# A decoder layer with routed experts on one core: routing's last row sends and its two counts are moved

## The chip, the cores and the metric

The kernel runs on one core of one Trainium2 chip. Times are device microseconds (us) of a whole execution; lower is better. Three runs of the kernel before took 683.22, 685.04 and 685.03 us, a median of 685.03. The execution that the profiler recorded took 685.55 us, of which 683.7 us lie between its first and last instruction (the span). Engines are called PE (TensorE), DVE (VectorE), ACT (ScalarE), POOL (GpSimd) and SP (SyncE, which here only issues transfers and loads registers from memory).

## The reference

Input x has 64 sequences of 64 tokens with 128 features, so 4096 rows, or 32 tiles of 128 rows. The layer does three things in a row: self-attention and a layer norm, cross-attention to a context and a layer norm, and a mixture of experts with a final layer norm. What matters here is the last part:

```python
t = (x * rsqrt(mean(x * x) + 1e-5) * norm_scale).reshape(4096, 128)
logits = t @ gate_w + gate_b                   # 8 experts
top_v, top_i = top_k(logits, 2)                # each row goes to 2 of them
probs = softmax(top_v)
h = swiglu(t @ w1[e] + b1[e])                  # 128 -> 512 -> 256
y = h @ w2[e] + b2[e]                          # 256 -> 128
x = layernorm(x + sum of probs * y over the row's two experts)
```

## The kernel before, in words

The kernel has two stages. In the first, attention and cross-attention run over the 32 tiles as a software pipeline: every engine has its own instruction list, written as one slot per step (`slot(at)`), with waits on semaphores between the engines. A cross-attention step works on several tiles at once, each at its own lag: at step s the layer norm's scale is made for tile s-10 (POOL, L1012, then the residual's bias for tile s-9, L1017), the normed row for tile s-11 (DVE, L1153), the router's logits for tile s-14. There are 60 such steps, 0 to 59; the last tile's scale is made at step 41, and steps 42 to 49 only finish the routing.

Routing collects tiles in batches of 8, 8, 4, 4, 4 and 4. For a batch, DVE chooses two experts per row in four phases (L1089 to L1174), PE sums how many rows went to each expert so far (L887 to L893), and DVE makes each row's place in a table in memory sorted by expert (`x_pos`, L1131, semaphore `placed`). POOL then sends the rows there: `send_row` issues indirect transfers of 128 rows each (L778, `disp_dram<-l_R,x_pos`), two for a tile, one for each choice. A list made when the program is built, `scatter_at`, says how many at which step; what is left (`late`, tiles 24 to 31) is sent inside the next stage.

The rows are sorted in two parts: tiles 0 to 19 are the first, 20 to 31 the second. When a part's batches are counted, PE makes the totals (`tally`, L917) and DVE a table of which block of 128 sorted rows belongs to which expert (`count`, L1197, and `table`, L1203 to L1218; SP stores it, L768). For the second part this is followed by two instructions that make `l_c`, a factor per row.

The second stage runs over 48 pairs of blocks of 128 sorted rows. For a pair, SP loads two table entries into registers (`find`, L1327) and issues two loads of 128 rows (`m_blk<-disp_dram`, L1339); for the first pair it first waits until the first part's 40 sends have landed (`scattered[0]`). PE loads the two experts' numbers (`load_experts`, L1370), turns the blocks (`turn_rows`, L1378), and multiplies (L1397, L1403, then L1412, L1422, and L1433 to turn the middle result). DVE divides a turned pair into a high and a low part (`split`, L1556 and L1561), then makes `m_lin` (L1610), `m_pr` (L1615) and the product (L1622). POOL sends the results (L1535). Before its loop PE turns pairs 0 and 1, and inside the loop pair p+2 behind the first products of pair p; DVE likewise splits pairs 0 and 1 first, and pair p+2 between `m_pr` and the product of pair p. All orders are written out by hand; each engine runs its list strictly in that order.

Of the kernel before, what the change touches and what calls it, by code (L numbers as in the profile page):

```python
# [641 lines left out]
def cross_attention(nc, ctx, ps, x1, x1_stored, ctxT, biases, disp, block_table, tiles, later):  # L642
# [7 lines left out]
    BATCHES = ((0, 8), (8, 8), (16, 4), (20, 4), (24, 4), (28, 4))  # L650
# [3 lines left out]
    part_of = lambda B: 0 if B < firsts else 1  # L654
    scatter_at, sent = {}, 0
    for step in range(tiles + LAG):
        placed_tiles = sum(n for t, n in BATCHES if step >= t + n + 18)
        some = min(placed_tiles - sent, 1 if step < tiles + 10 else 4) if step < tiles + 14 else 0
        scatter_at[step] = range(sent, sent + some)
        sent += some  # L660
    late = range(sent, tiles)
    def sb(name, shape, dt=F32):
        return ctx.enter_context(nc.sbuf_tensor("x_" + name, shape, dt))

# [92 lines left out]
    def step_of(at):  # L757

        return at[0] * U + at[1]
# [7 lines left out]
        sp.wait_ge(table_made, 2 * part + 2)  # L767
        sp.dma_start(block_table[part * P:part * P + P, :], eri[:, part, :]).then_inc(later.table_stored[part], 16)  # L768

    def send_row(pool, t):  # L770

        B = batch_of[t]
        j = t - BATCHES[B][0]
        if t == 0:
            pool.wait_ge(later.pattern_made, 3)
        pool.wait_ge(placed, B + 1)
        for k_ in range(2):
            nc.gpsimd.indirect_dma_start(  # L778
                out=disp[:, :], out_offset=bass.IndirectOffsetOnAxis(ap=pos[:, B, k_, j:j + 1], axis=0),
                in_=R[:, t, k_, :], in_offset=None).then_inc(scattered[part_of(B)], 16)  # L780

    def sync(sp):
        def slot(at):
# [16 lines left out]
    def tensor(pe):  # L800
# [7 lines left out]
        def slot(at):  # L808
# [64 lines left out]
            before = Tile(at, 8)  # L873
            if before.live:
                before.wait(pe, normed)
            if step_of(at) == tiles + 10:
                pe.wait_ge(tally_read, 1)
            if o.live:
                o.free(pe, lg_kept, 1)
# [2 lines left out]
            if z.t in last_of:  # L882
# [11 lines left out]
                                            ohs[:, B % 2, i, :].unsqueeze(1).to_broadcast([P, size - 1 - i, 8]),  # L894
                                            start=False, stop=(i == size - 2), skip_group_check=True)
                last.then_inc(ranked, 1)
            if step_of(at) == tiles + 9:
                tally(0)
            if o.live:
                if o.t == 0:  # L900
# [11 lines left out]
        def tally(part):  # L912

            B = (firsts, len(BATCHES))[part]
            pe.wait_ge(rank_read, B)
            pe.wait_ge(counted, B + 1)
            nc.tensor.matmul(ps_cnt, later.onesb[:, :], cum[:, B + part, :], start=True, stop=True).then_inc(tallied, 1)  # L917

        return slot, lambda: tally(1)

    def scalar(act):
        def slot(at):
# [68 lines left out]
    def gpsimd(pool):  # L991
        G = nc.gpsimd
        pool.wait_ge(later.filled, later.all_filled)

        def slot(at):
            c, h, k, w = (Tile(at, n) for n in (3, 9, 10, 2))
            if c.live:
                if c.t == 0:
                    pool.wait_ge(prepared, 4)
                c.wait(pool, k_ready)  # L1000
                c.free(pool, scored, 3)
                G.tensor_tensor(  # L1002
                    KB[:, c.t % 3, :, :, :],
                    kT[:, c.u4, :].rearrange("p (b k) -> p b k", b=2).unsqueeze(2).to_broadcast([P, 2, 8, T]),
                    hm[:, :].unsqueeze(1).unsqueeze(3).to_broadcast([P, 2, 8, T]),
                    ALU.mult).then_inc(k_spread, 1)
            if k.live:
                k.wait(pool, ln_var)
                if k.t == 0:
                    G.iota(R[:, :, :, P:P + 1].rearrange("p t k o -> p t (k o)").bitcast(I32), [[1, tiles], [CAP, 2]],  # L1010
                           base=0, channel_multiplier=32).then_inc(later.pattern_made, 1)
                G.tensor_tensor(later.rs[:, k.t, :], ve[:, k.u2, :], later.halfneg[:, 0:2],  # L1012
                                ALU.pow).then_inc(ln_rstd, 1)
            if h.live:
                h.wait_ring(pool, xb_in, 16)
                h.free(pool, y_added, 2)
                G.tensor_tensor(xr[:, h.u2, :], xb[:, h.u2, :], bob[:, :], ALU.add).then_inc(residual, 1)  # L1017
            if 0 <= w.t < 8:
                e = w.t
                pool.wait_ge(W1_cut, e + 1)  # L1020
                G.tensor_tensor(later.W1l[:, e, :], later.W1[:, e, :], W1c[:, e % 2, :],
                                ALU.subtract).then_inc(later.W1_low, 1)
            for t in scatter_at[step_of(at)]:
                send_row(pool, t)
        return slot, lambda: None

    def vector(dve):
# [16 lines left out]
        def slot(at):  # L1044
# [16 lines left out]
            if o.live:  # L1061
# [1 line left out]
                oB = batch_of[o.t]  # L1063
                V.tensor_tensor(lg[:, oB % 2, o.t - BATCHES[oB][0], :], ps_lg, later.gb[:, :],
                                ALU.add).then_inc(lg_kept, 1)
            if step_of(at) == tiles + 10:
                count(0)
            if rank:
                yB = last_of[y.t]
# [119 lines left out]
            if w.t == 18:  # L1189
                dve.wait_ge(B_part, 2)  # L1190
                V.tensor_tensor(Brest[:, 1, :], Brest[:, 0, :], Bpart[:, 1, :], ALU.subtract).then_inc(B_rest, 1)
            if step_of(at) == tiles + 10:
                table(0)
        def count(part):

# [30 lines left out]
            n.settle()  # L1226
            n.add(V.scalar_tensor_tensor(later.c2[:, :], later.rs[:, :, 0], 2.0, later.c2[:, :], ALU.mult, ALU.mult))

        return slot, end

    return sync, tensor, scalar, gpsimd, vector, store_table, late, send_row

# [1 line left out]
def experts(nc, ctx, ps, disp, block_table, Y, out, tiles, later, store_table, late, send_row):  # L1234
# [54 lines left out]
    def part_of(p):  # L1289

        return 0 if p < PA else 1
# [70 lines left out]
    def tensor(pe):  # L1362
# [19 lines left out]
        load_experts(1)  # L1382
        turn_rows(0)
        turn_rows(1)
        for s in range(PAIRS + 2):
            p, q, u = s, s - 2, s - 1
            if p < PAIRS:
# [123 lines left out]
    def gpsimd(pool):  # L1511
# [15 lines left out]

        for q in range(PAIRS):
            for t in late[0:3] if q == 0 else late[3 + q // 2:4 + q // 2] if q % 2 else ():
                send_row(pool, t)  # L1530
            pool.wait_ge(y_ready, q + 1)
            if q >= 4:
                pool.wait_ge(*landed(q - 4))
# [12 lines left out]
    def vector(dve):  # L1546
# [58 lines left out]

        split(0)
        split(1)
        for p in range(PAIRS):
            dve.wait_ge(up, p + 1)
            n.add(V.tensor_scalar(lin[:, :, :], ps_l[:, p % 2, :, :], -6.0, 8.0, ALU.max, ALU.min))  # L1610
# [146 lines left out]
```

## Time and profile before

| | |
|---|---|
| median of three runs | 685.03 us (683.22 to 685.04) |
| the profiled execution | 685.55 us, span 683.7 us |
| busy, share of the span | PE 78%, DVE 72%, POOL 65%, ACT 63% |
| last steps of the first stage (414 to 438 us) | DVE busy 16.57 of 24 us, POOL 19.84, PE 15.16 |
| from there to the first expert products (438 to 469 us) | PE busy 3.15 of 31 us, DVE 11.38, POOL 23.27 |
| the stretch from 482.4 to 640 us | PE busy 138.46 of 157.6 us |

Busy time is not the same as what sets the end: between 438 and 469 us no engine but POOL has much to do, and the time passes in waits. A timeline row gives the start, the duration, the engine, the line of the kernel and, in brackets, how long the engine stood idle before it and what ended that. The chain of waits follows the work that ended last back from the end, and names at each moment the engine or transfer it hung on.

### The profile page before, as it was taken

To read this page: it belongs to the slowest core of one execution; us is meant where nothing else is said; L and a number is where in the kernel's file an instruction comes from. 1 tells how busy PE (TensorE), PEld (TensorE's weight loads), DVE (VectorE), ACT (ScalarE), POOL (GpSimd) and SP (SyncE) were. 2 spreads that over 40 slices of the span, in tenths; PEclk is the share of its full clock that TensorE was granted. 3 is DMA by queue.
4 is the path that set the end of the run, shared out by engine and by line. 5 is a ranking of instruction groups with operands and counts; after the bars stand their busy time and mean duration, and the time that the engine had idled before them with its cause. 6 is when DMAs were issued, how large, how long until landed. Compare 5 with 4: busy or idle time off the path is not lost.

```text
span 683.7 us, 18235 instructions
## 1 busy us (share of the span) xinstructions
PE 535.7 (78%) x5390; PEld 415.6 (61%) x5390; DVE 489.7 (72%) x1696; ACT 430.6 (63%) x1287; POOL 445.9 (65%) x475
## 2 busy tenths in 40 slices
PE   7678779688886769999989888403887899999962
PEld 3456656566665646777756666302776788888830
DVE  3689896689998776878898987732554666678813
ACT  3799888789996759778756654101434555555633
POOL 6678796678896596566558886873265445456742
PEclk9899998899998989999999989555899999999998
DMA  2255655745222111111112111121222222252144
GB/s 58 88 196 192 231 192 160 259 122 144 51 58 63 54 47 33 37 35 49 37 34 59 36 33 45 44 61 49 55 63 65 63 63 64 55 178 62 47 117 121
DMA packets 72528, 58.48 MB, mean 86 GB/s; under 512 B 22866, under 2 KB 66012, under 8 KB 70386
## 3 DMA queue, kind: packets, MB, share of 16 engines
q1 hardware_dynamic: 67250, 47.79, 23.9%
q0 software_dynamic: 4608, 8.47, 3.8%
q10 hardware_dynamic: 576, 1.05, 0.5%
q8 instruction: 48, 0.79, 0.5%
q14 instruction: 46, 0.38, 0.2%
HBM read 26.39 MB, written 31.92 MB: 85 GB/s over the span
## 4 chain that ended last, share of the span: by engine, by line
PE 31%; issue 19%; POOL 15%; ACT 10%; DVE 9%; DMA 8%; SPq 6%; another core or an unknown queue 1%; ACTq 0%; DVEq 0%; POOLq 0%
PE ps L1397 9%; POOL l_keys L1002 6%; DMA l_shifted<-in_xT 5%; ACT l_weights L359 5%; PE ps L1422 4%; POOL disp_dram L778 4%; PE ps L1403 2%; PE ps L320 2%; POOL l_rs L1012 2%; PE ps L1433 2%; SPq L242 2%; POOL x_xr L1017 2%; PE ps L290 1%; PE ps L313 1%
## 5 line engine op out<-in xcount | busy, mean ns | idle before, releaser
L1535 POOL DMA_INDIRECT y_dram<-l_keys,m_blk x80 | 79.4, 992 | 89.3 <-ACT l_keys L1485 71.1
L359 ACT ACTIVATE l_weights<-ps,a_nb,a_rinv 128x64 f32<-128x64 f32 x256 | 99.5, 414 | 4.5 <-DVE a_nb L480 3.7
L778 POOL DMA_INDIRECT disp_dram<-l_R,x_pos x64 | 63.1, 987 | 17.5 <-issue 17.0
L446 POOL TENSOR_TENSOR a_rinv<-a_ms,a_halfneg 128x10 f32<-128x10 f32 (+1 forms) x32 | 62.5, 1953 | 11.0 <-DVE a_ms L512 8.9
L1610 DVE TENSOR_SCALAR m_lin<-ps 128x512 f32<-128x512 f32 x40 | 27.7, 692 | 50.7 <-PE ps L1403 48.0
L320 PE MATMUL ps<-l_R,l_shifted 128*128 128x512 f32 x64 | 40.5, 717 | 28.2 <-DMA l_shifted<-in_xT 19.7
L1002 POOL TENSOR_TENSOR l_keys<-x_kT,l_table 128x1024 f32<-128x1024 f32 x32 | 61.1, 1908 | 0.2
L1485 ACT ACTIVATE l_keys<-ps,m_blk 128x128 f32<-128x128 f32 x80 | 25.0, 363 | 49.6 <-PE ps L1422 33.3
L359 ACT ACTIVATION_READ_ACCUMULATOR l_weights<-ps,a_nb,a_rinv 128x1 f32 x256 | 55.2, 216 | 0.0
L1012 POOL TENSOR_TENSOR l_rs<-x_ve,l_halfneg 128x2 f32<-128x2 f32 x32 | 25.6, 799 | 39.9 <-DVE x_ve L1149 39.3
L412 POOL TENSOR_TENSOR l_R<-l_weights,a_pa 128x512 f32<-128x512 f32 x32 | 33.5, 1046 | 26.3 <-DVE a_pc L574 24.4
L1397 PE MATMUL ps<-l_W1h,m_th 128*128 x160 | 37.8, 318 | 15.1 <-issue 9.2
L1422 PE MATMUL ps<-l_table,l_keys 128*128 x320 | 43.1, 277 | 4.9 <-ACT l_keys L1498 3.3
L1477 ACT ACTIVATE l_weights<-ps 128x512 f32<-128x512 f32 x40 | 23.9, 598 | 35.9 <-PE ps L1403 32.7
L1105 DVE TENSOR_REDUCE x_mx<-ps 128x16 f32<-128x1024 f32 x32 | 39.0, 1219 | 7.8 <-PE ps L832 7.8
L1422 PEld LDWEIGHTS ps<-l_table,l_keys 128*128 128x128 f32 x320 | 38.8, 191 | 6.4 <-issue 6.4
L1397 PEld LDWEIGHTS ps<-l_W1h,m_th 128*128 128x128 f32 x160 | 26.2, 196 | 23.9 <-issue 23.8
L832 PE MATMUL ps<-l_keys,x_qT 64*64 64x512 f32 x256 | 36.4, 640 | 5.2 <-DVE l_shifted L1127 4.8
L932 ACT ACTIVATE l_weights<-l_shifted 128x1024 f32<-128x1024 f32 x32 | 33.6, 1050 | 10.0 <-DVE l_shifted L1127 9.9
L1127 DVE TENSOR_TENSOR l_shifted<-ps,x_mx 128x1024 f32<-128x1024 f32 x32 | 38.7, 1208 | 0.2
L909 PE MATMUL ps<-l_VB,x_PT 128*64 128x32 f32 x1024 | 36.8, 226 | 0.6 <-ACT x_PT L937 0.6
L332 PE MATMUL ps<-l_R,l_W1h 128*128 128x256 f32 x128 | 36.0, 405 | 1.3 <-ACT l_R L347 1.3
(229 smaller groups left out, 1728.6 us busy)
## 6 DMA issues: line engine op xcount, KB each, us to landing
disp_dram<-l_R SPq DMA_DIRECT2D x16, 1040.0 KB, 4.4
m_blk<-disp_dram SPq DMA_DIRECT2D x80, 65.0 KB
l_shifted<-in_xT SPq DMA_DIRECT2D x32, 64.0 KB, 3.9
l_W1h<-v_dram SPq DMA_DIRECT2D x128, 16.0 KB, 2.3
l_R<-in_x SPq DMA_DIRECT2D x32, 64.0 KB, 2.1
x_dram<-a_xo SPq DMA_DIRECT2D x32, 64.0 KB, 1.7
l_W1l<-in_w SPq DMA_DIRECT2D x4, 512.0 KB
x_xa<-x_dram SPq DMA_DIRECT2D x32, 64.0 KB, 1.8
```

The costliest lines, as they stand in the source:

```text
L320: nc.tensor.matmul(flat[:, 0:512], xTt[:, a.u2, :], wqkv[:, 0:512], start=True, stop=True)
L359: last = nc.scalar.activation(E[:, e.u4, g, :], ps_Sh[:, g % 2, g // 2, 0:D], ACT.Exp, bias=nb[:, e.u2, g:g + 1], scale=rinv[:, e.u4, g:g ...
L446: G.tensor_tensor(rinv[:, b.u4, 0:w], ms[:, b.u2, 0:w], halfneg[:, 0:w], ALU.pow).then_inc(inv_rms, 1)
L778: nc.gpsimd.indirect_dma_start(out=disp[:, :], out_offset=bass.IndirectOffsetOnAxis(ap=pos[:, B, k_, j:j + 1], axis=0), in_=R[:, t, k_, :] ...
L909: last = nc.tensor.matmul(ps_O[T * q:T * q + T, c, :], PT[:, c, T * q:T * q + T], VB[:, f.u4, q, c, :], start=True, stop=True)
L1002: G.tensor_tensor(KB[:, c.t % 3, :, :, :], kT[:, c.u4, :].rearrange("p (b k) -> p b k", b=2).unsqueeze(2).to_broadcast([P, 2, 8, T]), hm[: ...
L1012: G.tensor_tensor(later.rs[:, k.t, :], ve[:, k.u2, :], later.halfneg[:, 0:2], ALU.pow).then_inc(ln_rstd, 1)
L1105: n_mx = n.add(V.tensor_reduce(mx[:, :], ps_S, AX.X, ALU.max))
L1127: V.tensor_tensor(sh[:, d.u2, :, :], ps_S, mx[:, :].unsqueeze(2).to_broadcast([P, H, T]), ALU.subtract).then_inc(shifted, 1)
L1397: nc.tensor.matmul(dst[:, p % 2, j, :], left, right[:, bass.ds(e, 1), half * I:(half + 1) * I].rearrange("p a n -> p (a n)"), start=(i == ...
L1422: last = nc.tensor.matmul(ps_y[:, j, :], hT[:, q % 2, 2 * j + c, :], W2[:, bass.ds(expert[2 * q + j], 1), c, :].rearrange("p a n -> p (a n)"),
L1535: G_.indirect_dma_start(out=Y[:, :], out_offset=bass.IndirectOffsetOnAxis(ap=blk[:, (2 * q + j) % NB, P:P + 1].bitcast(I32), axis=0), in_= ...
```

## The change

Three edits, with no instruction added or removed.

1. Sends are now counted in single transfers and not in tiles. Up to step 34 there are two a step as before; from step 35 to 41 three a step; from step 42 up to eight. Transfers 0 to 38 are then sent by step 41 (before: 0 to 31), 39 to 46 at step 42 (before: 32 to 39), 47 at step 43 (before: 40 to 47). The late ones stay.
2. The first part's total (PE), its `count` and its `table` (DVE) stand three steps sooner: PE at step 38, DVE at step 39.
3. The second part's total stands on PE behind the turn of pairs 0 and 1, and its count, table and `l_c` on DVE behind the split of pairs 0 and 1, ahead of the first `m_lin`.

```diff
-        placed_tiles = sum(n for t, n in BATCHES if step >= t + n + 18)
-        some = min(placed_tiles - sent, 1 if step < tiles + 10 else 4) if step < tiles + 14 else 0
+        placed_rows = 2 * sum(n for t, n in BATCHES if step >= t + n + 18)
+        most = 2 if step < tiles + 3 else 3 if step < tiles + 10 else 8 if step < tiles + 14 else 0
+        some = min(placed_rows - sent, most)
         scatter_at[step] = range(sent, sent + some)
         sent += some
-    late = range(sent, tiles)
+    late = range(sent // 2, tiles)
...
-    def send_row(pool, t):
+    def send_row(pool, row):
+        t, k_ = row // 2, row % 2
...
-        for k_ in range(2):
-            nc.gpsimd.indirect_dma_start(
+        nc.gpsimd.indirect_dma_start(
...
     def tensor(pe):
-            if step_of(at) == tiles + 10:
+            if step_of(at) == tiles + 7:
                 pe.wait_ge(tally_read, 1)
-            if step_of(at) == tiles + 9:
+            if step_of(at) == tiles + 6:
                 tally(0)
-        return slot, lambda: tally(1)
+        later.last_tally = lambda: tally(1)
+        return slot, lambda: None
...
     def vector(dve):
-            if step_of(at) == tiles + 10:
+            if step_of(at) == tiles + 7:
                 count(0)
-            if step_of(at) == tiles + 10:
+            if step_of(at) == tiles + 7:
                 table(0)
-        return slot, end
+        later.last_table = end
+        return slot, lambda: None
...
         turn_rows(0)
         turn_rows(1)
+        later.last_tally()
...
         split(0)
         split(1)
+        later.last_table()
```

The program's order on POOL, at the last steps of the first stage: `l_rs` and `x_xr` open a step's work, the sends close it. Before:

```order
L1012 TENSOR_TENSOR l_rs<-x_ve,l_halfneg 128x2
L1017 TENSOR_TENSOR x_xr<-x_xb,x_bob 128x128
L778 DMA disp_dram<-l_R,x_pos 33024x130 x2
L1012 TENSOR_TENSOR l_rs<-x_ve,l_halfneg 128x2
L778 DMA disp_dram<-l_R,x_pos 33024x130 x24
L1535 DMA y_dram<-l_keys,m_blk 8192x128 x2
```

And in the changed kernel:

```order
L1014 TENSOR_TENSOR l_rs<-x_ve,l_halfneg 128x2
L1019 TENSOR_TENSOR x_xr<-x_xb,x_bob 128x128
L779 DMA disp_dram<-l_R,x_pos 33024x130 x3
L1014 TENSOR_TENSOR l_rs<-x_ve,l_halfneg 128x2
L779 DMA disp_dram<-l_R,x_pos 33024x130 x18
L1540 DMA y_dram<-l_keys,m_blk 8192x128 x2
```

Each of steps 35 to 40 has a third send, and the run that closes step 41 (3, 8, 1 and the first 6 late ones) has 18 and not 24.

On DVE, between the last place of routing (`x_pos`) and the first `m_lin` of the experts, before:

```order
L1131 CAST x_pos<-x_posf 128x2x4
L1197 TENSOR_SCALAR x_ni<-ps 128x8
L1203 TENSOR_SCALAR x_nbi<-x_ni 128x8
...
L1218 TENSOR_SCALAR x_eri<-x_er,l_table 128x1
L1225 RECIPROCAL l_c<-l_rs 128x32
L1227 SCALAR_TENSOR_TENSOR l_c<-l_rs,l_c 128x32
L1556 TENSOR_SCALAR m_tTc<-ps 128x256
L1561 TENSOR_TENSOR m_tl<-ps,m_tTc 128x256
L1556 TENSOR_SCALAR m_tTc<-ps 128x256
L1561 TENSOR_TENSOR m_tl<-ps,m_tTc 128x256
```

And in the changed kernel:

```order
L1133 CAST x_pos<-x_posf 128x2x4
L1561 TENSOR_SCALAR m_tTc<-ps 128x256
L1566 TENSOR_TENSOR m_tl<-ps,m_tTc 128x256
L1561 TENSOR_SCALAR m_tTc<-ps 128x256
L1566 TENSOR_TENSOR m_tl<-ps,m_tTc 128x256
L1199 TENSOR_SCALAR x_ni<-ps 128x8
L1205 TENSOR_SCALAR x_nbi<-x_ni 128x8
...
L1220 TENSOR_SCALAR x_eri<-x_er,l_table 128x1
L1227 RECIPROCAL l_c<-l_rs 128x32
L1229 SCALAR_TENSOR_TENSOR l_c<-l_rs,l_c 128x32
L1616 TENSOR_SCALAR m_lin<-ps 128x512
```

The thirteen instructions of the second count now stand between the split of pair 1 and the first `m_lin`.

On PE the total `ps<-x_cum,l_onesb 128x8` of the second part stood ahead of the expert numbers' loads:

```order
L893 MATMUL ps<-x_ohs,l_onesb 128x8
L917 MATMUL ps<-x_cum,l_onesb 128x8
L1370 TENSOR_LOAD block_table
...
L1378 MATMUL ps<-l_table,m_blk 128x128 x4
L1397 ISA
```

and now stands behind both turns (the x4 are pairs 0 and 1):

```order
L894 MATMUL ps<-x_ohs,l_onesb 128x8
L1373 TENSOR_LOAD block_table
...
L1381 MATMUL ps<-l_table,m_blk 128x128 x4
L918 MATMUL ps<-x_cum,l_onesb 128x8
L1401 ISA
```

It can run only once pair 1's rows are there, since PE takes its list in order.

## Rows read from the trace of the kernel before

**Rows 1.** The page: shares of the chain that ended last, by engine.

```profile
PE 31%; issue 19%; POOL 15%; ACT 10%; DVE 9%; DMA 8%; SPq 6%; another core or an unknown queue 1%; ACTq 0%; DVEq 0%; POOLq 0%
```

**Rows 2.** Chain of waits, 444 to 476 us: start us, us, what.

```profile
440.49 3.58 DMA block_table<-x_eri
...
447.30 4.83 issue
...
452.29 0.36 SPq L1339
...
453.14 0.70 SPq L1339
...
471.38 0.69 SPq L1327
...
472.60 0.15 SPq L1327
...
473.54 1.87 DMA m_blk<-disp_dram
```

**Rows 3.** Timeline of PE, 441 to 479 us: start us, us, instruction, [idle before].

```profile
445.57 0.22 PE L893 MATMUL ps<-x_ohs,l_onesb 128*128 128x24 bf16 x3
446.79 0.17 PE L917 MATMUL ps<-x_cum,l_onesb 128*128 128x8 bf16 x1 [1.00 <-issue]
455.14 0.69 PE L1378 MATMUL ps<-l_table,m_blk 128*128 128x128 f32 x2 [8.18 <-DMA m_blk<-disp_dram]
468.77 0.69 PE L1378 MATMUL ps<-l_table,m_blk 128*128 128x128 f32 x2 [12.95 <-DMA m_blk<-disp_dram]
```

**Rows 4.** Timeline of POOL, 412 to 490 us.

```profile
417.00 0.96 POOL L778 DMA_INDIRECT disp_dram<-l_R,x_pos  x1 [0.30 <-issue]
418.88 0.82 POOL L1012 TENSOR_TENSOR l_rs<-x_ve,l_halfneg 128x2 f32<-128x2 f32 x1 [0.92 <-DVE x_ve L1149]
...
422.64 0.73 POOL L1012 TENSOR_TENSOR l_rs<-x_ve,l_halfneg 128x2 f32<-128x2 f32 x1
...
437.36 0.73 POOL L1012 TENSOR_TENSOR l_rs<-x_ve,l_halfneg 128x2 f32<-128x2 f32 x1
...
449.84 0.95 POOL L778 DMA_INDIRECT disp_dram<-l_R,x_pos  x1 [0.30 <-issue]
...
467.52 0.96 POOL L778 DMA_INDIRECT disp_dram<-l_R,x_pos  x1 [0.30 <-issue]
```

**Rows 5.** Timeline of DVE, 412 to 490 us.

```profile
431.31 0.29 DVE L1086 TENSOR_TENSOR x_r<-ps,x_xr 128x128 f32<-128x128 f32 x1 [1.93 <-POOL x_xr L1017]
...
438.63 0.17 DVE L1203 TENSOR_SCALAR x_nbi<-x_ni 128x8 int32<-128x8 int32 x1
...
447.32 0.16 DVE L1197 TENSOR_SCALAR x_ni<-ps 128x8 int32<-128x8 f32 x1
...
451.10 0.22 DVE L1227 SCALAR_TENSOR_TENSOR l_c<-l_rs,l_c 128x32 f32<-128x32 f32 x1 [0.95 <-DVE l_c L1225]
...
469.96 0.42 DVE L1561 TENSOR_TENSOR m_tl<-ps,m_tTc 128x256 fp32r<-128x256 f32 x1
472.64 0.69 DVE L1610 TENSOR_SCALAR m_lin<-ps 128x512 f32<-128x512 f32 x1 [2.25 <-PE ps L1403]
...
476.10 0.42 DVE L1556 TENSOR_SCALAR m_tTc<-ps 128x256 uint32<-128x256 uint32 x1 [2.04 <-PE ps L1378]
```

**Rows 6.** Busy time of each engine, granted clock and DMA share by stretch.

```profile
core 0: us, PE busy (x) PEld busy (x) DVE busy (x) ACT busy (x) POOL busy (x), PEclk, DMA share, GB/s
451.00:469.00 18.00, 0.91 (x3) 0.52 (x4) 1.07 (x3) 0.42 (x1) 13.41 (x14) 0.50 0.24 67
...
475.60:482.40 6.80, 5.53 (x25) 4.86 (x25) 2.64 (x5) 1.31 (x3) 0.00 (x0) 0.50 0.27 45
```

**Rows 7.** Chain of waits, 476 to 500 us.

```profile
477.33 2.93 PE ps L1397 x12
...
486.91 1.75 PE ps L1397 x12
```

More of the change, by code:

```diff
@@ L768, in store_table @@
         sp.dma_start(block_table[part * P:part * P + P, :], eri[:, part, :]).then_inc(later.table_stored[part], 16)
-    def send_row(pool, t):
+    def send_row(pool, row):
+        t, k_ = row // 2, row % 2
         B = batch_of[t]
         j = t - BATCHES[B][0]
-        if t == 0:
+        if row == 0:
             pool.wait_ge(later.pattern_made, 3)
         pool.wait_ge(placed, B + 1)
-        for k_ in range(2):
-            nc.gpsimd.indirect_dma_start(
-                out=disp[:, :], out_offset=bass.IndirectOffsetOnAxis(ap=pos[:, B, k_, j:j + 1], axis=0),
-                in_=R[:, t, k_, :], in_offset=None).then_inc(scattered[part_of(B)], 16)
+        nc.gpsimd.indirect_dma_start(
+            out=disp[:, :], out_offset=bass.IndirectOffsetOnAxis(ap=pos[:, B, k_, j:j + 1], axis=0),
+            in_=R[:, t, k_, :], in_offset=None).then_inc(scattered[part_of(B)], 16)
     def sync(sp):
@@ L1022, in slot @@
                                 ALU.subtract).then_inc(later.W1_low, 1)
-            for t in scatter_at[step_of(at)]:
-                send_row(pool, t)
+            for row in scatter_at[step_of(at)]:
+                send_row(pool, row)
         return slot, lambda: None
@@ L1529, in gpsimd @@
             for t in late[0:3] if q == 0 else late[3 + q // 2:4 + q // 2] if q % 2 else ():
-                send_row(pool, t)
+                send_row(pool, 2 * t)
+                send_row(pool, 2 * t + 1)
             pool.wait_ge(y_ready, q + 1)
```

## The prediction

> **What bounds the kernel now.** I read four views, in this order. The page's chain of waits comes first: it hangs on PE for 31% and on POOL for 15%, and 19% of it is "issue", time in which the engine at its head waited for nothing that the profile shows [rows 1]. So there is no single bound; the end is the sum of stages, and a change in one stage is worth what that stage gets shorter. Second, the chain in order of time between 444 and 476 us, where the change acts. There it runs through SP and not through a computing engine: SP has its table entries, stands for 4.83 us, issues pair 0's first load at 452.29 us, and then each instruction of its list shows about 0.70 us, from 453.14 to 471.38 us; right after that the same register operation takes 0.15 us [rows 2]. I call this stretch the slow spell. Third, PE's timeline: it is through with routing at 446.79 us, stands 8.18 us for pair 0's rows and 12.95 us more for pair 1's, which it turns at 468.77 us [rows 3]. No product can start before, since PE turns both pairs first. Fourth, POOL's timeline in the same time: it sends without a break up to 467.52 + 0.96 us [rows 4]. From 451 to 469 us PE, DVE and ACT are each busy for about 1 us or less of 18, POOL for 13.41, the rest of POOL's time being the gap that each send has before it [rows 6].
>
> So what bounds this stretch is the first part's 40th send. It is the one at 449.84 us, the last of step 42; SP's first load follows at 452.29, 2.45 us later [rows 2, 4]. Behind it, SP's slow spell sets when pair 1's rows come.
>
> **Edit 1, three sends a step.** What one send costs: the sends at 449.84 and 467.52 us are 14 apart, (467.52 - 449.84) / 14 = 1.263 us from start to start [rows 4]. Seven of them move from steps 42 and 43 to steps 35 to 41. If the steps had room for them, the 40th send would go out 7 x 1.263 = 8.8 us sooner; if they had none, not at all. These are the two ends. The rows tell which is near. POOL had 0.92 us idle ahead of step 36's scale (418.88 us) and none ahead of the one of step 37 (422.64 us) [rows 4]; and at 431.31 us it is DVE that stood 1.93 us for POOL's `x_xr` [rows 5]. From step 36 on POOL is the engine the others wait for, so a third send there only makes the step longer. Idle time that a third send can fill: the 0.92 us behind step 35's sends. The longer idle time ahead of step 35's scale lies before the first added send and stays. The gain is 0.92 us: the 40th send goes at 449.84 - 0.92 = 448.9 us, SP's first load at 451.4.
>
> What is late in exchange: step 41's scale stands behind six added sends now, 6 x 1.263 - 0.92 = 6.7 us later, at 437.36 + 6.7 = 444.0 us [rows 4]. DVE's steps 42 to 49 follow it, and with them PE's last sums, 445.57 + 6.7 = 452.2, less 1.9 us for the table that no longer stands among those steps (438.63 to its store at 440.49 [rows 2, 5]): 450.4 us. Then PE loads four experts' numbers; before, this ended well inside the 8.18 us that it stood [rows 3]. Even if it took 4 us it would be over at 454.4, against 455.14 - 0.92 = 454.2 for pair 0's turn: a tie, and harmless, because the products wait for pair 1's turn 13 us later. I take 0 for it. Every batch's places are made before POOL comes to the sends that need them.
>
> At this place the Trainium skill has a rule on how POOL is to be read. Its page "Perfetto Trace Analysis", section "GPSIMD Instruction", says that a GpSimd instruction's span in a profile is unreliable and is better timed by the spacing of starts. The rows bear it out: 0.95 to 0.96 us of span against 1.263 us of spacing. By spans the ends would be 6.7 us and 0, and the value taken would be the same 0.92.
>
> **The slow spell.** After step 42's first send there are 7 + 1 + 6 = 14 more, and behind step 42's last there were 8 + 6 = 14 before. So between SP's first load and the end of POOL's sends the program has the same list on both engines as before, all 0.92 us sooner. Pair 1's turn moves with it, to 467.9 us, and so does pair 2's load, whether the spell ends with the sends or lasts for a number of SP's instructions. This edit is worth -0.9 us to the end.
>
> **Edit 2, the first count three steps sooner.** The table's store goes from 440.49 to about 434 us. SP then stands longer for the 40 sends; the 4.83 us before [rows 2] become some 10. Worth 0. Its cost, 1.9 us of DVE at step 39, lies ahead of DVE's next wait for POOL, which was 1.93 us there [rows 5] and grows by 1.26 with the third send. Queued behind PE's wait for the reading of the total are the logits and the last products of step 39; they wait for one DVE instruction that stands early in the step. 0.
>
> **Edit 3, the second count behind pair 1.** Thirteen DVE instructions. They took from 447.32 to 451.10 + 0.22 us = 4.0 us before, with two unusual pauses; the same table for the first part took 1.9 us, with the count and the factor some 2.4 [rows 2, 5]. So between 2.4 and 4.0 us, and I take the dearer. Before, they stood in DVE's idle time ahead of pair 0, so taking them away gives nothing. At the new place: DVE ends pair 1's split at 469.96 + 0.42 - 0.92 = 469.5 us, the count ends at 473.5 at the latest, and the first `m_lin` starts there and not at 472.64 - 0.92 = 471.7. It is up to 1.8 us late. Behind it stand `m_lin` and `m_pr`, 2 x 0.7 = 1.4 us, and then pair 2's split, which waited 2.04 us for PE's turn and started at 476.10, now 475.2 [rows 5]. 473.5 + 1.4 = 474.9: through with 0.3 us to spare, 1.9 us with the cheaper value. ACT uses `l_c` only behind pair 2's split. The cover is that wait for pair 2's rows, and if it were gone, up to 4.0 us would stand open. On PE the total is one short product, 0.17 us [rows 3], ahead of pair 0's products: 0.2 us at most, within the rounding. Worth 0.
>
> **Sum.** -0.9 + 0 + 0 = -0.9 us. Against the profiled execution: 685.55 - 0.9 = 684.6, span 682.8. That execution is 0.5 us above the median, so for the median 685.03 - 0.9 = 684.1 us. From 482.4 us on nothing is changed, and the stretch moves as a whole.
>
> **The rivals.**
> *The slow spell gets shorter.* Before, SP's first load came some 11 sends into an unbroken run of 24; now it comes 5 sends into one of 18. If the spell needs a long run behind it, SP's loads for pair 1 are issued fast. For it: SP's steps were not slow in the steps with two sends. Against it: it began right behind SP's own first load, not at a number of sends. Without any spell, pair 1's rows come 2.5 us behind pair 0's and not 468.77 - 455.14 = 13.6; PE would turn them at about 457 us, 12 us sooner, and the second count's open time would be made up by pair 2's rows coming sooner too: 673 us. With half of it: 679. The Trainium skill speaks for a spell that has another cause: "DMA: Bandwidth & Descriptors", section "Issuing engines are not separate DMA queues", says that all transfers interleave on the same 16 engines whoever issues them. By it the sends could delay SP's data, hardly its register operations, and with a DMA share of 0.24 in the stretch [rows 6] not by much. The spell would then stay or go for reasons outside the sends; the time would be one of the two, 684.1 or 673.
>
> *The half clock lasts longer, and the kernel is slower.* The granted clock is at 0.50 (1.2 GHz) from 451 to 469 us, after little PE work, and still from 475.6 to 482.4 us [rows 6]. Twelve products take 2.93 us there and 1.75 us at full clock [rows 7]. Steps 36 to 41 now leave PE idler, and the level may return later. A pair costs 1.2 us more in these products and as much again, at most, in its turns and the rest: two more pairs at half clock are +3.8 us, so 685.03 - 0.9 + 3.8 = 687.9. It decides from the second such pair on; one alone gives +1.0, within 0.3%. Against it: the idle stretch ahead of pair 1 has the same length as before, and the steps that get idler end long before it.
>
> *It does what it says and POOL had room after all.* If a send costs less than 1.26 us of a step because DVE's chain is the longer one in steps 36 to 40, up to 8.8 us would be gained: 676 us. The rows at 422.64 and 431.31 us speak against it.
>
> **How the numbers follow.** About what this kernel's measurement can tell from no change is 0.3%, 2.1 us. Chances: my forecast 0.62, with an own range of 682.5 to 686; the shorter spell 0.20, a third of it as its full form; the longer half clock 0.14; room on POOL 0.04. Faster by over 0.3%: 0.20 + 0.04 and 0.06 of my forecast's spread, 0.30. Slower by over 0.3%: 0.14 and 0.02 of that spread, 0.16. Within: 0.54. The range leaves out the full form of the shorter spell and the far end of the half clock: 678 to 687.5.
>
> **What would show it.** Right: in the changed kernel the run behind step 41's scale has 18 sends; the scales of steps 36 to 41 stand about 5 us apart (before 3.7); SP's first `m_blk` load comes near 451.4 us; SP shows 0.70 us again; PE turns pair 1 near 467.9; DVE's second count ends about a microsecond or two behind PE's first products, and pair 2's split still waits for PE. Wrong: pair 1's turn before 465 us; SP's register operations at 0.15 us while POOL sends; DVE reaching pair 2's split later than its turn; a granted clock of 0.50 past 485 us.

## The result and the profile after

Both kernels were run 20 times in turn on one chip. The kernel before took 682.77 us (median, 678.88 to 685.67), the changed one 679.76 us (673.67 to 684.45): a ratio of 0.9954 with a 95% interval of 0.9932 to 0.9976. It is faster by 3.1 us, give or take 1.5. I had forecast 0.9 us. Repeated later on chip 2, 12 runs of the changed kernel had a median of 677.63 us against 683.44 for the one before, a ratio of 0.9921 (0.9887 to 0.9955). Both gains have the forecast's sign and are larger than forecast. The chip matters, as the experiments show, so each run below is named with its chip; the number of the first comparison's chip is not on record, and I call it the first chip. Ratios are of fast executions alone and are estimated together with their interval, so they can be up to 0.2% off the quotient of the medians.

The profiled execution of the changed kernel took 677.33 us, with a span of 675.5. Single executions of one kernel differ by 4 us before the change even begins to act: step 35's scale on POOL stands at 414.23 us in the first trace of before and at 410.05 in a second one; in this trace of the changed kernel it stands at 410.13. So all comparisons below count from step 35's scale. The second stage has 40 pairs, 0 to 39 (the traces have 40 `m_lin`), and not 48 as I wrote ahead of the prediction.

The chain's shares (the page, as [rows 1]). POOL's share fell from 15% to 12%, DMA's from 8% to 5%:

```profile
PE 33%; issue 20%; POOL 12%; ACT 11%; DVE 9%; SPq 6%; DMA 5%; another core or an unknown queue 2%; DVEq 0%; ACTq 0%; POOLq 0%
```

The timeline of POOL, which answers to [rows 4]:

```profile
415.16 0.73 POOL L1014 TENSOR_TENSOR l_rs<-x_ve,l_halfneg 128x2 f32<-128x2 f32 x1
...
420.06 0.74 POOL L1014 TENSOR_TENSOR l_rs<-x_ve,l_halfneg 128x2 f32<-128x2 f32 x1
...
439.84 0.73 POOL L1014 TENSOR_TENSOR l_rs<-x_ve,l_halfneg 128x2 f32<-128x2 f32 x1
...
444.76 0.96 POOL L779 DMA_INDIRECT disp_dram<-l_R,x_pos  x1 [0.30 <-issue]
...
462.43 0.96 POOL L779 DMA_INDIRECT disp_dram<-l_R,x_pos  x1 [0.30 <-issue]
```

The scales stand 4.9 us apart with no idle time ahead of them; before, it was mostly 3.7. The 40th send comes 444.76 - 410.13 = 34.63 us behind step 35's scale; before, 449.84 - 414.23 = 35.61. That is 0.98 us sooner.

The chain of waits in order of time, which answers to [rows 2, 7]:

```profile
429.77 0.32 SPq L769
...
435.81 11.30 issue
...
447.27 0.36 SPq L1342
...
448.52 0.70 SPq L1342
...
461.19 0.69 SPq L1342
...
462.58 2.95 DMA m_blk<-disp_dram
...
467.78 2.92 PE ps L1401 x12
```

The first table is stored at 429.77 us and SP stands 11.30 us for the sends, not 4.83. Its first load then goes out 2.51 us behind the 40th send (2.45 before). From 448.52 us on SP shows the 0.70 us again.

The timeline of PE, as [rows 3]:

```profile
446.40 0.22 PE L894 MATMUL ps<-x_ohs,l_onesb 128*128 128x24 bf16 x3
451.06 0.69 PE L1381 MATMUL ps<-l_table,m_blk 128*128 128x128 f32 x2 [4.44 <-issue]
457.31 0.69 PE L1381 MATMUL ps<-l_table,m_blk 128*128 128x128 f32 x2 [5.56 <-DMA m_blk<-disp_dram]
457.79 0.21 PE L918 MATMUL ps<-x_cum,l_onesb 128*128 128x8 bf16 x1
...
465.90 0.69 PE L1381 MATMUL ps<-l_table,m_blk 128*128 128x128 f32 x2 [4.38 <-DMA m_blk<-disp_dram]
```

Here is what I had not forecast. Pair 0's turn stands where it was (40.93 us behind step 35's scale, 40.91 before), but pair 1's follows 6.25 us later and not 13.63.

The timeline of DVE, as [rows 5]:

```profile
458.49 0.42 DVE L1566 TENSOR_TENSOR m_tl<-ps,m_tTc 128x256 fp32r<-128x256 f32 x1
458.83 0.15 DVE L1199 TENSOR_SCALAR x_ni<-ps 128x8 int32<-128x8 f32 x1
...
461.13 0.26 DVE L1229 SCALAR_TENSOR_TENSOR l_c<-l_rs,l_c 128x32 f32<-128x32 f32 x1
466.27 0.69 DVE L1616 TENSOR_SCALAR m_lin<-ps 128x512 f32<-128x512 f32 x1 [4.88 <-remote]
```

The second count takes 461.39 - 458.83 = 2.56 us and is through while PE makes pair 0's products, whose last group begins at 460.57 and runs 0.95 us. But `m_lin` starts only at 466.27. "remote" means that the wait ended with nothing that the profile can name. The trace's semaphore events can: PE's increment of `up` is recorded at 466.25 us, 4.73 us behind the end of the matmul that carries it, and the slow spell on SP is over at 466.1. Part of the time won is lost again there. `m_lin` of pair 0 starts 56.14 us behind step 35's scale (58.41 before), pair 1's 61.49 (66.95), and the end comes at 265.40 (269.52).

The busy time by stretch, as [rows 6]:

```profile
core 0: us, PE busy (x) PEld busy (x) DVE busy (x) ACT busy (x) POOL busy (x), PEclk, DMA share, GB/s
447.00:457.30 10.30, 0.69 (x2) 0.29 (x2) 1.96 (x9) 0.42 (x1) 7.65 (x8) 0.50 0.32 78
457.30:461.20 3.90, 3.89 (x18) 3.58 (x19) 2.89 (x15) 1.70 (x2) 2.91 (x4) 0.50 0.15 51
461.30:464.60 3.30, 0.22 (x2) 0.00 (x0) 0.09 (x1) 0.00 (x0) 1.78 (x2) 1.00 0.27 81
464.70:471.40 6.70, 4.31 (x19) 3.64 (x20) 2.73 (x5) 1.31 (x3) 0.00 (x0) 0.50 0.18 40
```

Two sets of twelve products run at a granted clock of 0.50 (1.2 GHz), one before and one after a short full stretch, as in the kernel before. The half clock doesn't last longer.

### The profile page after: what moved, and what is told of

Same layout as the page of the kernel before. It is cut to its first block, busy times and chain, and to the rows that moved or that the text cites. A ratio compares the mean times of both kernels' runs of the same rounds, so it can differ in the third digit from the quotient of the medians.

```text
span 675.5 us, 18237 instructions
## 1 busy us (share of the span) xinstructions
PE 536.7 (79%) x5390; PEld 417.1 (62%) x5390; DVE 489.1 (72%) x1696; ACT 430.4 (64%) x1287; POOL 445.9 (66%) x475
## 4 chain that ended last, share of the span: by engine, by line
PE 33%; issue 20%; POOL 12%; ACT 11%; DVE 9%; SPq 6%; DMA 5%; another core or an unknown queue 2%; DVEq 0%; ACTq 0%; POOLq 0%
PE ps L1401 8%; POOL l_keys L1004 6%; ACT l_weights L359 6%; PE ps L1426 4%; DMA l_shifted<-in_xT 4%; PE ps L1407 3%; POOL disp_dram L779 2%; PE ps L320 2%; PE ps L1437 2%; SPq L242 2%; PE ps L313 2%; PE ps L290 2%; PE ps L302 2%; POOL x_xr L1019 1%
## 5 line engine op out<-in xcount | busy, mean ns | idle before, releaser
L910 PE MATMUL ps<-l_VB,x_PT 128*64 128x32 f32 x1024 | 38.4, 231 | 0.8 <-ACT x_PT L939 0.6
L939 ACT ACTIVATE x_PT<-ps 128x1024 f32<-128x1024 f32 x32 | 32.6, 1017 | 8.7 <-PE ps L822 8.2
```

Of the source, the lines that this page charges most:

```text
L910: last = nc.tensor.matmul(ps_O[T * q:T * q + T, c, :], PT[:, c, T * q:T * q + T], VB[:, f.u4, q, c, :], start=True, stop=True)
```

## The experiments

Twelve runs on three chips. The table has medians; "end" is the end of the profiled execution, counted from step 35's scale. In the first chip's traces it is 269.52 us for before and 265.40 for after.

| run | chip | us | before, same chip | ratio (95%) | end |
|---|---|---|---|---|---|
| edit 1 alone | 3 | 682.93 | 683.07 | 1.0007 (0.9974-1.0040) | 272.42 |
| edits 2 and 3 alone | 3 | 682.26 | 683.07 | 0.9987 (0.9952-1.0021) | 277.34 |
| changed, late rows one a pair | 3 | 683.71 | 683.07 | 1.0016 (0.9988-1.0043) | 271.79 |
| changed, with pauses | 3 | 670.65 | 683.07 | 0.9823 (0.9783-0.9863) | 258.65 |
| before, with pauses | 7 | 649.60 | 650.91 | 0.9996 (0.9959-1.0033) | 238.97 |
| changed, pauses, second count early | 7 | 649.96 | 650.91 | 0.9976 (0.9936-1.0017) | 237.31 |
| changed, every second pause | 7 | 649.53 | 650.91 | 0.9971 (0.9933-1.0010) | 238.19 |
| changed, late sends paused too | 7 | 651.33 | 650.91 | 1.0004 (0.9967-1.0040) | 239.94 |
| changed, again | 2 | 677.63 | 683.44 | 0.9921 (0.9887-0.9955) | 267.55 |
| before, with pauses, again | 2 | 677.08 | 683.44 | 0.9894 (0.9844-0.9945) | 262.50 |
| before against itself | 3 | 681.73 | 682.73 | 1.0006 (0.9973-1.0039) | 274.84 |
| changed, with pauses, again | 3 | 668.17 | 682.73 | 0.9797 (0.9754-0.9840) | 258.96 |

**Edit 1 alone.** The counts stay where they were.

```diff
-            if step_of(at) == tiles + 7:
+            if step_of(at) == tiles + 10:
                 count(0)
```

> The changed kernel with its first edit alone: three sends a step, both counts where they were before. Theory 1 (the gain comes from POOL's sends: the 40th one is 0.9 us sooner and the unbroken run behind it is 18 long and not 24, which makes SP's slow spell shorter) expects the whole gain here: about 3 us under the kernel before, SP's first row load 0.9 us sooner counted from step 35's scale, and pair 1 turned at least 3 us sooner counted the same way. Theory 2 (the gain comes from taking the second count out of DVE's and PE's lists ahead of pair 0) expects the kernel before's time, within 1 us.

Measured: no gain, 1.0007. The trace shows where it goes. Its 40th send comes as early as in the changed kernel (34.65 us behind step 35's scale), but the longer steps delay the first table. The chain of waits:

```profile
441.60 0.32 SPq L769
...
448.73 0.69 SPq L1340
...
449.45 0.70 SPq L1340
```

The table's store goes out 441.60 - 408.74 = 32.9 us behind step 35's scale (26.3 before, 19.6 in the changed kernel). SP has then to read it, and its first load comes at 40.71, 6.06 us behind the 40th send and not 2.5. So in this trace edit 1 needs edit 2. The medians alone do not settle it, as the changed kernel without pauses was never timed on chip 3. And SP shows 0.69 us here at 448.73 us already, before its first load is out: the spell does not begin with that load.

**Edits 2 and 3 alone.**

```diff
-        most = 2 if step < tiles + 3 else 3 if step < tiles + 10 else 8 if step < tiles + 14 else 0
+        most = 2 if step < tiles + 10 else 8 if step < tiles + 14 else 0
```

> The changed kernel with both moved counts, but two sends a step up to step 41 as before. Theory 1 expects no gain: within 1 us of the kernel before, SP's slow spell as long as before, the second count hidden by DVE's wait. Theory 2 expects 3 us less than before.

Measured: 0.9987, no gain that can be told from none. Its 40th send is late, 39.02 us behind step 35's scale where the first trace of before had 35.61. Two steps are longer than in that trace; the same is seen below in two traces of kernels without edit 1.

**Late rows one a pair.** In five of the loop's pairs POOL has four sends in a row, and ACT waits up to 3.1 us for "remote" there. Here each pair gets one late row at most.

```diff
+            first = 2 * late[0]
+            for row in range(first, first + 6) if q == 0 else range(first + 5 + q, first + 6 + q) if q < 11 else ():
+                send_row(pool, row)
```

> The changed kernel, but the ten late row sends that went out two at a time behind the results of pairs 0, 2, 4, 6 and 8 go out one at a time, behind the results of pairs 0 to 9. In both traces PE's semaphore increments come about 2 to 2.5 us late in each of the five pairs with two row sends, which follow two result sends: four sends in a row. Theory A (it takes four sends at 1.26 us from start to start to build this up) expects that no increment is late with three in a row: up to 5 x 2 = 10 us less than the changed kernel. Theory B (what counts is how many row sends there are, wherever they stand) expects the same time within 1 us, with ten smaller delays.

Measured: 1.0016, 4 us slower by the ratio than the changed kernel was on the first chip; part of that may be the chip. Up to `m_lin` of pair 0 it is like the changed kernel (56.28 us), and from pair 1's to pair 39's it takes 169.6 us where the two traces of the changed kernel have 166.9 and 166.6. Increments still come 1 to 3.7 us late, most of them in every second pair. Four sends in a row are not the condition.

**The changed kernel with pauses.** An addition that nobody reads (0.41 us) stands behind the sends of rows 39 to 53.

```diff
+        if 39 <= row < 54:
+            nc.gpsimd.tensor_tensor(pause[:, row - 39, :], bob[:, :], bob[:, :], ALU.add)
```

> The changed kernel with a small POOL addition (128x128 into a buffer that nobody reads) behind each of rows 39 to 53's sends, so that these sends stand about 1.7 us apart and not 1.26, while SP loads pairs 0 and 1. Number of sends and of SP's instructions unchanged. Theory A (the sends' pace at 1.26 us makes SP slow) expects SP's register operations at their 0.15 us, pair 1 turned 3 to 6 us sooner than in the changed kernel counted from step 35's scale, and 2 to 5 us less in total. Theory C (SP is slow in this stretch whenever any sends are under way, or for its own loads' sake) expects pair 1's turn where it was or later, and the time within 1 us or longer.

Measured: 0.9823, 12.4 us faster than before. The timeline of POOL:

```profile
444.18 0.41 POOL L785 TENSOR_TENSOR x_pause<-x_bob 128x128 f32<-128x128 f32 x1
444.76 0.98 POOL L781 DMA_INDIRECT disp_dram<-l_R,x_pos  x1 [0.17 <-issue]
445.77 0.41 POOL L785 TENSOR_TENSOR x_pause<-x_bob 128x128 f32<-128x128 f32 x1
446.35 0.98 POOL L781 DMA_INDIRECT disp_dram<-l_R,x_pos  x1 [0.17 <-issue]
```

and of PE:

```profile
450.06 0.69 PE L1385 MATMUL ps<-l_table,m_blk 128*128 128x128 f32 x2 [4.71 <-issue]
451.57 0.69 PE L1385 MATMUL ps<-l_table,m_blk 128*128 128x128 f32 x2 [0.82 <-DMA m_blk<-disp_dram]
```

The sends start 1.585 us apart and not 1.263; POOL is through 4.4 us later, and pair 1's turn follows pair 0's after 1.5 us. The spell on SP is gone but for a few instructions. PE's late increments are not: four of them, of matmuls that end between 470.8 and 472.5 us, are recorded 3.8 to 5.3 us late, and `m_lin` of pair 4 waits 6.34 us for "remote".

**The kernel before with pauses, and three variants of the paced kernel.** These four ran on chip 7.

> The kernel before with the same pause (a 128x128 addition on GpSimd) behind the sends of rows 39 to 53, so that they stand 1.585 us apart there too. If the slow spell comes from the sends' pace, it goes here as well, and what is left between this kernel and the paced changed one is the worth of the three edits without the spell. Theory P (the edits are worth what the blind sum said, 0.92 us of sends, less the second count, which now stands open for some 2 us): this kernel at 683 - 12 = 671, within 1.5 us of the paced changed kernel's 670.65. Theory Q (the three edits themselves are worth the measured 3 us): 674. Theory R (the shorter run of sends is what made the changed kernel quicker, and the pause does the same for both): 671, and pair 1's turn 1.5 to 2.5 us behind pair 0's.

```diff
+            if 39 <= 2 * t + k_ < 54:
+                nc.gpsimd.tensor_tensor(pause[:, 2 * t + k_ - 39, :], bob[:, :], bob[:, :], ALU.add)
```

> The paced changed kernel with the second part's count back at the end of routing (edit 3 undone). There PE and DVE turn and split pair 0 and 1 at once and the count's 2.6 us are no longer hidden behind a wait for rows. If it was open in the paced kernel, moving it back ahead of pair 0's rows, into idle time, makes m_lin of pair 0 start 2 to 2.6 us sooner and the kernel 2 us faster, about 668.5. If the first m_lin's start is set by PE's products (11 us behind the turn) or by pair 2's rows, nothing is gained: 670.6.

```diff
-        later.last_table = end
-        return slot, lambda: None
+        return slot, end
```

> The paced changed kernel with the pause behind every second send only (rows 39, 41, ... 53): pairs of sends 1.26 us apart, 1.42 us on the mean. If the spell depends on the mean pace with a limit between 1.26 and 1.42, it is gone and the time is 670 or a little less, since POOL is through 2.2 us sooner. If only the full 1.585 us lets the queue drain, SP shows 0.70 us again for a part of the stretch and the time lies between 672 and 679.

```diff
-        if 39 <= row < 54:
+        if 39 <= row < 54 and row % 2:
```

> The paced changed kernel with the pause behind the late sends too (rows 39 to 63, the ten in the loop included). In the five pairs of the loop with two row sends, four sends follow each other at 1.27 us and two pairs took 10.2 us where others took 8.2. If pace is the cause there as well, this costs nothing on POOL, which waits 3 us for ACT once every two pairs, and gains up to 5 x 2 = 10 us: 661. If those 2 us have another cause (ACT's or PE's own work), 670 to 671; if POOL becomes late by its pauses, 1 to 2 us slower.

```diff
-        if 39 <= row < 54:
+        if 39 <= row < 64:
```

Measured: the kernel before, without any pause, takes 650.91 us on this chip, 32 us less than on the others, and none of the four differs from it by more than its interval. Most of my expectations miss, as they took the spell for a property of the program. Up to step 35's scale all is as long as elsewhere (407.45 to 411.48 us here, 408.51 to 414.23 on the others). What is missing is the lateness. I matched each of PE's 684 semaphore increments with its own record in the trace. In the first trace of before 28 are recorded over 0.7 us behind their matmul and 35 have no record of their own, in the one of the changed kernel 38 and 34, and over all ten traces of the other chips 28 to 50 and 28 to 55. In the four traces of chip 7 none is late, and 0, 2, 0 and 0 have no record. In each of the ten, PE's first missing record stands 1.5 to 1.7 us behind POOL's first send of rows, at 358.3 to 363.2 us, and none is late or missing before it.

The pauses do not change this on a chip that has it: the two traces of the changed kernel with pauses on chip 3 have 38 and 40 late increments and 55 and 43 without a record. So the late increments and SP's slow list are two things, and only the second went with the pauses. All four kernels profiled on chip 7 have pauses; the kernel before without any was timed there and not profiled, but it is as quick as they are. And all runs on chip 7 were made in one session, so what is said of the chip could be of the occasion. From `m_lin` of pair 1 to that of pair 39 it is 150.4 us in the paced kernel before, against 166.4 in the first trace. The page shows it in how long POOL stood idle ahead of its sends of results (behind the second bar: in all, and what of it ended with ACT's results), for the kernel before on the first chip (first fence) and with pauses on chip 7 (second):

```profile
L1535 POOL DMA_INDIRECT y_dram<-l_keys,m_blk x80 | 79.4, 992 | 89.3 <-ACT l_keys L1485 71.1
```

```profile
L1540 POOL DMA_INDIRECT y_dram<-l_keys,m_blk x80 | 80.0, 1000 | 50.7 <-ACT l_keys L1490 31.2
```

The same on SP's timeline. Its first ten loads of rows take 26.64 us on the first chip in the kernel before, and 11.63 us on chip 7 in the kernel with every second pause, though sends 1.26 us apart are among them:

```profile
452.29 26.64 SPq L1339 DMA_DIRECT2D m_blk<-disp_dram  x10
```

```profile
448.57 11.63 SPq L1346 DMA_DIRECT2D m_blk<-disp_dram  x10
```

Is it the rows' data? The trace's packets of the software queue speak against it: on the first chip and on chip 7 the first packet of a send leaves mostly 1.53 to 1.61 us behind the send's start, in the spell too. The Trainium skill, page "DMA: Bandwidth & Descriptors", section "Issuing engines are not separate DMA queues", has all transfers interleave on the same engines. I take from it that contention would show as late packets, and those of the sends aren't late. What is late is instructions on SP and semaphore increments of engines.

The early second count tells what edit 3 costs when rows come promptly. The timelines of DVE, with the count early:

```profile
449.87 0.41 DVE L1232 SCALAR_TENSOR_TENSOR l_c<-l_rs,l_c 128x32 f32<-128x32 f32 x1
...
455.22 0.69 DVE L1616 TENSOR_SCALAR m_lin<-ps 128x512 f32<-128x512 f32 x1 [2.40 <-PE ps L1408]
```

and with the count behind pair 1 (the kernel with late sends paused too, which is the paced kernel up to here, on the same chip):

```profile
455.22 0.25 DVE L1233 SCALAR_TENSOR_TENSOR l_c<-l_rs,l_c 128x32 f32<-128x32 f32 x1
455.40 0.68 DVE L1620 TENSOR_SCALAR m_lin<-ps 128x512 f32<-128x512 f32 x1
```

With the count early DVE waits 2.40 us for PE's products; with it late it waits for nothing and `m_lin` starts 47.03 us behind step 35's scale against 46.65. Even without a wait for rows the products cover all of it but 0.4 us, and the two medians can't be told apart.

**The changed kernel again, and the kernel before with pauses again**, both on chip 2.

> The changed kernel, nothing altered. The kernel before took 683 us on one chip and 650.9 us on another; all kernels profiled on the quick one had pauses. If the quick chip is one on which the slow spell does not exist (theory N), a run there shows pair 1's turn 1.5 to 2 us behind pair 0's and no 0.70 us instructions on SP without any pause, and the three edits are worth what the sends give, 0.92 us, plus or minus: within 1.5 us of the kernel before at 651. If the spell is there on every chip and only pauses remove it, PE stands over 5 us for pair 1. If this lands on a chip where the kernel before takes 683: the ratio to it is 0.995 again (679.8).

> The kernel before with the pause behind the sends of rows 39 to 53, once more. On a chip where the kernel before takes 683 us it tells whether pauses remove the slow spell from it as they did from the changed kernel: 671 (the spell comes of the pace), or 683 (something in the changed kernel was needed too). On a chip where it takes 651: 649.5 to 651 again, since there is nothing to remove.

Measured: 0.9921 and 0.9894. Here the spell is there. In the changed kernel pair 1's turn follows pair 0's after 6.12 us, nearly as in its first trace. In the paced kernel before it is 4.91 us, and SP still shows some 0.70 us: 7 us were gained of the 12 expected. Its 40th send is late (38.86 us), by the same two longer steps as above. So pauses alone took off 1.1%, the edits alone 0.8% on the same chip, and both together 1.8% on chip 3: about their sum.

**The kernel before against itself, and the paced kernel again**, both on chip 3.

> The kernel before, unaltered, against itself. Its ratio must hold 1 in its interval; how far it is off tells how much the other ratios are to be trusted. On a chip where it takes about 683 us: PE stands 13 us for pair 1 and PE's and ACT's semaphore increments are up to 5 us late, as in its first trace. On a chip where it takes about 651 us: theory N (the spell belongs to the chip and needs no pause to be absent) says that pair 1's turn comes 2 to 3 us behind pair 0's and that no instruction on SP takes 0.70 us in that stretch though the sends stand 1.26 us apart; theory P (the pace makes the spell on every chip) says that PE stands over 8 us for pair 1.

> The changed kernel with the pause behind the sends of rows 39 to 53, once more, since it was timed in one call only. If its 12 us were the pauses' on chips that show the spell: 0.980 to 0.990 of the kernel before on such a chip, less than 0.992 (the changed kernel's there). On a chip without the spell: the same within 2 us, about 650.

Measured: 1.0006 and 0.9797. The first holds 1 in its interval, as it should. Its trace is of use too. The timeline of POOL:

```profile
410.05 0.82 POOL L1012 TENSOR_TENSOR l_rs<-x_ve,l_halfneg 128x2 f32<-128x2 f32 x1 [0.96 <-DVE x_ve L1149]
...
416.23 0.82 POOL L1012 TENSOR_TENSOR l_rs<-x_ve,l_halfneg 128x2 f32<-128x2 f32 x1 [2.45 <-DVE x_ve L1149]
...
429.11 0.82 POOL L1012 TENSOR_TENSOR l_rs<-x_ve,l_halfneg 128x2 f32<-128x2 f32 x1 [1.85 <-DVE x_ve L1149]
```

and of DVE:

```profile
427.02 0.26 DVE L1060 RECIPROCAL x_rz<-ps 128x16 f32<-128x16 f32 x1 [3.83 <-PE ps L909]
```

Two steps take 6.18 and 5.48 us where [rows 4] have 4.65 and 3.7: DVE waits for PE. The increment that ends this wait is recorded 0.89 us behind its matmul, half of what the step is too long; the other half I can't name. The 40th send comes 38.82 us behind step 35's scale, 3.2 us later than in the first trace. So it is in three of the four traces of kernels without edit 1 on chips with the spell, and in none of the six with edit 1. There POOL is busy without a gap. Late increments come in these kernels too (in the first trace of the changed one PE's at 413.82 us is recorded 2.10 us late, and DVE starts right behind the record), yet the scales stay 4.9 us apart: as I read it, the delay is used up in the waiting of PE and DVE for POOL.

The second repeats the pauses' effect: 14.6 us by the medians, 12.4 the first time. Of all kernels run on chips 2 and 3 it is the fastest.

## Why the prediction came out as it did

The forecast's sign was right and its size too small: -0.9 us, measured -3.1 and, on chip 2, a ratio of 0.9921. The stated range, 678 to 687.5 us, holds the measured 679.76, but only since it was drawn wide for the rivals; my forecast's own 682.5 to 686 does not hold it. Of the 4.3 us between the forecast 684.1 and 679.76, 2.3 are the base: I counted from a median of three executions, 685.03 us, and twenty gave 682.77. Point by point.

**The price of a send and the gain of edit 1** were right against the execution I read: 1.263 us a send, steps 4.9 us apart, 0.98 us measured for 0.92 forecast. Right too were what goes with it, step 41's scale 29.7 us behind step 35's (forecast 29.8) and the first table's store 19.6 (forecast some 20). As a mean over executions this term was mis-sized. My sum stood on one profiled execution, and in it the two long steps did not occur. Over the two traces of before, SP's first load comes 38.06 and 41.27 us behind step 35's scale; over the two of the changed kernel 37.14 and 37.16. That is 2.5 us on the mean, 0.9 of it from sends and 1.6 from steps that POOL's work now covers.

**Edit 2 "worth 0"** was wrong, by leaving out how edits hang together. I checked what the third send does to DVE's steps and to PE, not what it does to the table that SP needs. Edit 1 alone was worth nothing (1.0007): in its trace SP waits for the table. Edits 2 and 3 alone show no gain either (0.9987). That the whole is worth more than its parts is read from these traces; the times of the parts and of the whole come from different chips.

**The slow spell "moves with it".** This is the step that failed: "between SP's first load and the end of POOL's sends the program has the same list on both engines as before", so all of it 0.92 us sooner. The list is the same and its timing isn't. From pair 0's turn to pair 1's it was 13.6 and 11.4 us in the two traces of before, 13.3 with edit 1 alone, 8.6 with edits 2 and 3 alone, 6.25 and 6.1 in the changed kernel, 5.3 in the one with late rows one a pair. The spell ends 3.6 and 2.7 us behind the run of sends (57.8 us behind step 35's scale before, 56.0 in the changed kernel), and what changed is how far SP gets in it: its fourth load, pair 1's last, goes out at 55.75 us before and at 45.46 in the changed kernel. So my rival of a shorter spell happened in part. That its half form said 679 us and 679.76 was measured is luck: it meant 6 us off a base of 685, and 3.1 off 682.8 were measured. Most of the 7 us between the turns was not kept. `m_lin` of pair 0 stood 4.88 us for PE's late increment, and pair 2's rows still came late, so that 2.3 us were left at `m_lin` of pair 0, and over both traces of each kernel 3.7 there, 5.9 at pair 1's and 5.7 at the end. My reason against that rival, that the spell begins with SP's first load, fell with the first experiment, where it began before.

**Edit 3** was right: 2.56 us of DVE, hidden. I had named the wait for pair 2's rows as its cover and up to 4.0 us as the price without it. With that wait gone, 0.4 us stood open, since PE's own products cover it as well.

**The longer half clock** did not come: the clock is 0.50 for the same number of product sets. **Room on POOL** was not there: no idle time ahead of the scales from step 36 on.

What stays open. Why some chips show late increments, missing records and slow SP instructions at all, and chip 7 almost none, can't be told from here. Why SP gets more instructions through in the spell in the changed kernel also stays open. It goes together with how long SP had stood before its first load: 0.7 us in edit 1 alone, 4.8 and 4.6 before, 13.8 and about 11 us in the kernels with edit 2. That is a correlation over few traces; a kernel that changes this wait alone wasn't tried. Whether the late sends of the loop should be paced too was tried only on the chip where it can't help.

## What to carry to other kernels

Before an edit is priced from one trace, look whether the waits it leans on recur in a second execution: here 1.6 of the 2.5 us at SP's first load lay in delays that the first trace happened not to have. When work is moved forward behind a wait for two things, check the other of the two as well; in these traces the earlier sends paid only together with the earlier table. And when a run of indirect transfers goes with slow instructions elsewhere, try to put a little distance between them: 15 idle additions of 0.41 us took 7 us off the kernel before and some 9 us more off the changed one, and on a chip without the trouble they cost nothing that could be measured.

## What the runs showed of the hardware that was not expected

The same kernel takes 683 us on chips 2 and 3 and 651 us on chip 7, with the same time up to step 35's scale and a mean granted clock of 0.91 to 0.94 on each. What the traces show different behind it are late semaphore increments and SP's 0.70 us instructions. They are two things. SP's depend on the pace of POOL's indirect sends: at 1.263 us from start to start its list crawls, at 1.585 us it runs in the changed kernel (two traces) and crawls for a shorter time in the kernel before (one trace). PE's late and missing increments begin 1.5 to 1.7 us behind the first indirect send and come with and without pauses: 28 to 50 late of 684, none on chip 7. Of the eight runs on chips 2 and 3, six had medians from 677 to 684 us, and only the two of the changed kernel with pauses came to 671 and 668.
